# A few waits and positions moved in a projection, block-attention and linear kernel

## The reference

```
n = layernorm(x); q, k, v = n@Wq+bq, n@Wk+bk, n@Wv+bv        # split into heads
local: query block i of 128 attends to keys [128 i - 64, 128 i + 192), softmax
global: tokens {0, 62 of largest |q|, 1023} of every head attend to all 1024 keys
        and their rows replace the local ones
x = x + attention;  out = x + layernorm(x) @ (weight * scale[:, None]).T + bias
```

## Time and profile before

| | |
|---|---|
| median of three runs | 2026.45 us |
| the profiled execution, its own time | 2021.86 us |
| its span | 2020.2 us |
| PE busy (matmuls) | 1975.3 us, 98% |
| DVE busy | 1507.7 us, 75% |
| ACT busy | 1045.3 us, 52% |
| POOL busy | 543.3 us, 27% |
| granted TensorE clock, mean | 0.997 of full speed |
| one 128x512 matmul in a projection | about 0.25 us from start to start |

### The profile page before, as it was taken

How to read it: one execution, slowest core, us unless ns; L and a number is a source line. 1 busy time by engine, 2 the same in 40 slices (tenths; PEclk the granted TensorE clock), 3 DMA queues, 4 the chain that set the end, 5 groups by cost and what they waited for, 6 DMA issues and landing times.

```text
span 2020.2 us, 36804 instructions
## 1 busy us (share of the span) xinstructions
PE 1975.3 (98%) x11264; PEld 1646.0 (81%) x11264; DVE 1507.7 (75%) x2917; ACT 1045.3 (52%) x1483; POOL 543.3 (27%) x430
## 2 busy tenths in 40 slices
PE   6999999999999999999999999999999999999999
PEld 6877888888778888888788888888888888888887
DVE  5597788865877888658778887587777887666664
ACT  4326766773267667732676677327777770000100
POOL 2333123134331221243312212433222213112211
PEclk9999999999999999999999999999999999999999
DMA  3447777764377777643677776337777664333331
GB/s 126 145 113 135 157 157 159 144 126 144 119 134 158 156 161 145 123 142 122 130 161 157 161 144 125 111 92 135 157 165 172 138 149 173 125 139 132 134 127 70
DMA packets 533830, 280.79 MB, mean 139 GB/s; under 512 B 433264, under 2 KB 498870, under 8 KB 533680
## 3 DMA queue, kind: packets, MB, share of 16 engines
q1 hardware_dynamic: 505584, 186.76, 43.7%
q0 software_dynamic: 23776, 76.63, 11.7%
q10 hardware_dynamic: 4320, 15.73, 1.9%
HBM read 122.73 MB, written 51.44 MB: 86 GB/s over the span
## 4 chain that ended last, share of the span: by engine, by line
PE 62%; DVE 15%; DMA 7%; issue 7%; ACT 3%; POOL 2%; SPq 2%; DVEq 1%; ACTq 0%; POOLq 0%
PE proj L678 30%; PE proj L839 16%; PE pv L797 6%; DMA p_turned<-p_parts 5%; DVE p_parts L1564 2%; DVE top_idx L1520 2%; PE pv L819 2%; DVE x_norm L1522 2%; PE score L785 2%; PE turn L785 2%; DVE top_val L1518 1%; SPq L295 1%; PE turn L828 1%; ACT pT L1176 1%; PE proj L953 1%
## 5 line engine op out<-in xcount | busy, mean ns | idle before, releaser
L678 PE MATMUL proj<-xT_hi,w_lo 128*128 128x512 f32 x1536 | 417.6, 400 | 0.0
L678 PE MATMUL proj<-xT_hi,w_hi 128*128 128x512 f32 x1536 | 402.9, 404 | 4.9 <-POOL w_lo L468 2.4
L678 PE MATMUL proj<-xT_lo,w_hi 128*128 128x512 f32 x1536 | 385.7, 393 | 0.0
L678 PEld LDWEIGHTS proj<-xT_lo,w_hi 128*128 128x128 f32 x1536 | 291.0, 190 | 65.7 <-DVE xT_lo L1478 1.0
L1176 ACT COPY pT<-p_turned 128x1024 uint16<-128x1024 uint16 x256 | 331.7, 1373 | 21.4 <-DMA p_turned<-p_parts 21.1
L678 PEld LDWEIGHTS proj<-xT_hi,w_lo 128*128 128x128 f32 x1536 | 281.1, 190 | 58.6
L678 PEld LDWEIGHTS proj<-xT_hi,w_hi 128*128 128x128 f32 x1536 | 274.4, 188 | 63.4 <-issue 3.6
L1564 DVE COPY p_parts<-probs 128x1024 uint16<-128x1024 uint16 x320 | 225.2, 725 | 109.5 <-DMA p_turned<-p_parts 57.8
L523 POOL TENSOR_TENSOR w_lo<-w_raw,w_hi 128x1024 fp32r<-128x1024 f32 x48 | 120.2, 2505 | 593.6 <-DVE q_sq L1554 326.4
L797 PEld LDWEIGHTS pv<-v_nat,pT 128*128 128x128 f32 x2048 | 246.9, 191 | 22.5 <-issue 12.3
L797 PE MATMUL pv<-v_nat,pT 128*128 128x65 f32 x2048 | 244.2, 272 | 6.7 <-DVE ctx_out L1600 5.9
(11 more groups left out here) (181 smaller groups left out, 3173.1 us busy)
## 6 DMA issues: line engine op xcount, KB each, us to landing
w_raw<-in_wstream POOLq DMA_DIRECT2D x94, 512.0 KB, 3.7
x_buf<-in_rows SPq DMA_DIRECT2D x41, 512.0 KB, 3.3
q_rows<-pT SPq DMA_DIRECT2D x64, 256.0 KB, 2.4
ctx_rows<-ctx_out SPq DMA_DIRECT2D x128, 128.0 KB, 2.0
out<-q_store ACTq DMA_DIRECT2D x30, 512.0 KB, 2.6
q_store<-in_cols POOLq DMA_DIRECT2D x28, 512.0 KB, 5.3
q_store<-ctx_rows SPq DMA_DIRECT2D x28, 512.0 KB, 4.1
x_buf<-in_rows POOLq DMA_DIRECT2D x14, 512.0 KB, 6.5
```

What stands on the lines that cost most here:

```text
L678: mm = pe.matmul(proj[:, bank, :], w[b][:, k * P:k * P + P], x[:, k, half * HALF:half * HALF + HALF], start=(m == 0), stop=(m == 23), skip ...
```

## The change

It does five things, and no arithmetic is changed.

1. The POOL wait `parted_p(n, 0, 0)` ahead of `split_pair(n, "k", 1)` is gone, in all four batches.
2. The POOL wait `parted_p(n, PAIRS - 2, 2)` ahead of the bias additions is gone (batch 3).
3. The two `normalise` of the ahead tiles stand one place earlier in pair 6 (batch 3).
4. `ahead_hi(0)` on ACT stands behind `join_p(n, 6, 3)`, and `ahead_lo(0)` on DVE behind `columns(4)` (batch 3).
5. `spread_stats` issues both broadcasts in one place, ahead of `store_ctx(n, 3, 1)` and `turn_p(n, 3, 4)`, and waits for the whole of `top_rows` (batches 0 to 2).

```diff
         AHEAD_AT = {(5, 0): ("add", 0), (5, 1): ("moments", 0), (5, 3): ("add", 1), (5, 4): ("moments", 1),
-                    (6, 0): ("roots", 0), (6, 1): ("roots", 1), (6, 3): ("normalise", 0), (6, 4): ("normalise", 1)}
+                    (6, 0): ("roots", 0), (6, 1): ("roots", 1), (6, 2): ("normalise", 0), (6, 3): ("normalise", 1)}
...
-            def spread_stats(n, i):
-
-                if i == 0:
-                    sp.wait_ge(stat_out, n * 64 + 64)
-                    apart(sp)
-                    sp.wait_ge(top_step, n * (2 * TOP_LINKS) + TOP_LINKS + TOP_STEPS)
-                    apart(sp)
-                sp.dma_start((mean_b, rstd_b)[i], stat_rows[n, i].partition_broadcast(P)).then_inc(stat_in, 16)
+            def spread_stats(n):
+
+                sp.wait_ge(stat_out, n * 64 + 64)
+                apart(sp)
+                sp.wait_ge(top_step, (n + 1) * (2 * TOP_LINKS))
+                apart(sp)
+                for i, dst in enumerate((mean_b, rstd_b)):
+                    sp.dma_start(dst, stat_rows[n, i].partition_broadcast(P)).then_inc(stat_in, 16)
...
                 if hp == HALF_PAIRS - 1:
                     if following:
-                        spread_stats(n, 0)
+                        spread_stats(n)
                     else:
                         spread_scale(n)
                 store_ctx(n, hp, 1)
                 turn_p(n, hp, STEPS)
-                if hp == HALF_PAIRS - 1 and following:
-                    spread_stats(n, 1)
                 store_ctx(n, hp, 2)
...
                 load_columns(n, 0)
-                parted_p(n, 0, 0)
                 split_pair(n, "k", 1)
                 gather(n, 0)
...
                     pool.wait_ge(bias_in, 16)
-                    parted_p(n, PAIRS - 2, 2)
                     for b in range(AHEAD):
                         add_bias_ahead(n, b)
...
                 columns(4)
+                join_p(n, hp, STEPS - 1)
                 if early and not following:
                     ahead_hi(0)
-                join_p(n, hp, STEPS - 1)
                 out("k", 1, 3)
...
                 pv_out(u, 2)
+                columns(4)
                 if hp == PAIRS - 2 and not following:
                     ahead_lo(0)
-                columns(4)
                 if not last:
                     k_lo_out(n, hp + 1, 1)
```

## The result

The changed kernel takes 2041.52 us (median of 6 runs, 2035.65 to 2047.75), the kernel before 2025.90 in 6 runs beside it: ratio 1.0079, 95% interval 1.0056 to 1.0100. That is slower by 0.79%, outside the predicted range and on the side that had a chance of 0.12. The profiled execution took 2047.63 us with a span of 2046.0, the slow end of its kernel's own spread, against 2021.86 and 2020.2 before, the fast end of that one's: its 25.8 us are more than the 15.6 between the medians.

A forecast was written before the change was run, and what follows sets the result against it. The prediction took PE's own stream in program order (busy 1975.3 of 2020.2 us) to bound the kernel. Its terms, -0.3 + 0 + 2.4 + 1.6 + 0 = +3.7 us, gave a median of 2030.1 us, range 2019 to 2039.

The forecast's parts named there:

- What bounds it: Whole kernel: PE's stream in program order sets the time; edits count only through PE's waits and the clock behind them.
- Part 1: POOL wait removed at the start of attention, batches 0 to 2: -0.3 us, bounds -3.2 to +6.8.
- second rival: Start of attention: POOL takes the port before DVE's copies, second copy 3.4 us late; +11.8 us, 2038.3 in all; chance 0.13.
- about equally near: Batches 1 and 2, start of attention: wait's gain won, or DVE's copies delayed up to 3.4 us; taken as nothing.
- some 1 to 2: Start of attention: of a 3.4 us delay of DVE's second copy, 1 to 2 us would be seen at PE.
- Part 2: POOL wait removed ahead of batch 3's bias additions: 0 for PE, -0.7 to +0.9 us shift for later operations.
- they meet the two copies of pair 6, step 1: Batch 3: the earlier bias additions may make a second DVE copy 2 us late, hidden from PE.
- The expected gain: Batch 3: DVE's column scale no longer loses 1.9 us to the bias additions and takes 1.22 us.
- Part 3: Ahead tile in batch 3: ahead_lo(0) ends later, so PE's ahead projection starts 2.4 us later; bounds +0.5 to +3.3.
- Part 4: Second statistics broadcast beside the transposes of turn_p(3, 4): 0 us, bounds -0.4 to +1.0 in each of three batches.
- so a microsecond more should be hidden: Transposes of turn_p(3, 4): a microsecond's delay is hidden, as PE needs the result only mid-step 1 of the next pair.
- The clock: Behind PE's new 2.8 us wait at batch 3's ahead projection: one fall of the clock, +1.6 us, bounds 0 to 1.7.

The follow-up runs named there:

- e1: Kernel before without its POOL wait at the start of attention, nothing else changed: 2030.07 against 2024.85 us, ratio 1.0023.
- e7: Kernel before with the POOL wait ahead of batch 3's bias additions set on the end of DVE's small layer norm operations: 2026.45 against 2026.51 us, ratio 1.0002.
- e3: Kernel before with only ahead_hi(0) moved behind join_p(3) and ahead_lo(0) behind columns(4): 2028.57 us, ratio 1.0016.
- e2: Kernel before without its POOL wait ahead of the two bias additions of batch 3, nothing else changed: 2030.83 us, ratio 1.0027.
- e4: Kernel before with both statistics broadcasts issued in one place, the old looser wait for top_rows kept: 2027.44 us, ratio 1.0017.
- e8: Kernel before with pair 0's row moments on DVE moved behind pv_out(2): 2022.05 against 2025.36 us, ratio 0.9978.
- e9: Kernel before with pair 0's row moments behind pv_out(2), first POOL wait gone and key split ahead of load_columns: 2020.01 against 2025.36 us, ratio 0.9973.
- e5: Kernel before with its first POOL wait gone and the key split moved ahead of load_columns: 2026.47 against 2026.51 us, ratio 1.0003.
- e6: Changed kernel with the two layer norms of the ahead tiles back in their old places: 2042.77 us, ratio to the kernel before 1.0081.

## Why the prediction was wrong

**What bounds it** held: PE's stream in order, and waits with clock falls behind them. The sum of terms was wrong, +3.7 against +15.6.

**Part 1** was costed at -0.3, and measured +4.7 alone. The mechanism, its place and its size were in the text (3.4 us late; it was 3.0), as the second rival, with 0.13. The failed step is the choice between two cases "about equally near": I set batches 1 and 2 at nothing. But the choice was not open in that way: I had taken a tenth of a microsecond as what decides, and in batch 0 POOL won although the first copy's record starts 0.41 us ahead of the cast's. With two POOL operations against two copies, the offsets that the traces show, from 0.41 us one way to 0.11 the other, all collide. Batch 0 itself I had priced at a gain of 0.3 to 0.7, from copies that are nearly done when POOL comes free; they had hardly begun. What PE sees in batch 1 is two waits for `pT`, 1.34 and 1.56, in place of one of 1.84 for `q_pad`, and a longer fall of the clock, together 1.8 us of the 3.0 by which the copies are late. In batch 2 the changed kernel's trace shows next to nothing and e1's 2.7, so how much comes through differs by the execution; on the mean the "some 1 to 2" of the prediction fits the 4.7 us of e1 for three batches.

**Part 2** was costed at 0 (-0.7 to +0.9), and measured +5.5 alone. This is the largest miss. The step that failed is "they meet the two copies of pair 6, step 1". I had their new start right (1591.4), and then set it against the copies, which begin 1.8 us later, and not against the row at 1591.01: `ln_bits`, one of the operations that stand ahead of `maxima`. e7, which lets this stage of small operations pass first, has none of the loss. The expected gain did come: the column scale takes 1.22 us.

**Part 3** held: "PE starts at about 1622.2 instead of 1619.79: +2.4 us", and +1.6 for the clock, 4.0 together. e3 measured 2.3 more waiting, one fall, +4.1 in its trace and 3.2 us (1.0 to 5.5) in the medians' ratio. In the whole change the wait is 1.99.

**Part 4** was costed at 0 (up to +1.0 in each batch), and measured +3.4 alone. The place was right: the global product, which reads `pT_g`, stands in the middle of the next pair's step 1, and it is what waits. The failed step is "so a microsecond more should be hidden": the prediction shows no row of PE for it. In the trace of before the copy ends at 305.46 + 2.87 = 308.33 and PE is at this product at 308.92, so 0.6 us could be hidden. The transposes came about 1.9 us later (2.04 us of idle time on ACT against 0.16), so 1.3 was left in each batch.

**The clock** was given one fall in the sum, for the longest new wait alone. In their profiles e2 and e3 each have a fall of 3.4 us behind their new wait, and the falls of e1 are longer (17.0 us at half clock in all against 10.2); e4 has none behind its new waits.

**Open.** The 5.1 us in pair 1 of batch 2 stand behind the transpose that landed late (DVE waited 6.88 us for it). Of the eleven traces four have such a wait in this place: the changed kernel, e2 (6.56), e8 (6.17) and e9 (4.83). e2 touches nothing before batch 3, so I take it for something that comes in some executions of any of these kernels, and not for a cost of the change; that, and why it comes, was not tried. The last 3.1 us have a fall of 6.8 us at 1682.6 behind waits of 0.87 and 0.73 us, which the trace of before has alike, without a fall. Both belong to the 25.8 us of the two traces, and not for certain to the 15.6 between the medians.

## What to carry to other kernels

A wait of one engine may stand for two things, data and distance; before it goes, lay the operations that it will let loose over the other engine's rows at the new start time, by what stands in the row at that microsecond, the 0.17 us ones first, and with half a microsecond of slack either way. Follow a delayed result to the matmul that reads it, and take the difference of the two times for what can be hidden. Where waits of PE come in a cluster, taking the first away can give nothing (e5), where taking away the one behind it, which brings the clock down, does (e8).

## What the runs showed of the hardware

A 128x2 operation of DVE, 0.17 us long by itself, was held 5.15 us by two POOL additions in a row (e2 and the changed kernel alike; 5.17 in e6), though its record starts 0.37 us ahead of the first, so it would have been over. In both kernels, and at the copy of batch 0 (155.15), the held operation starts while POOL issues a DMA and the holding one is next behind that issue (155.56, 1604.38). In the traces of before and of e7 `ln_bits` started inside the same kind of issue, with POOL's next operation still waiting for a semaphore, and took 0.17. It looks as if POOL's next operation claims the port before its record starts; only these rows speak for it. The section that the prediction cites (the Trainium skill, SBUF — State Buffer, "Who interferes with whom") says that whoever issues first gets the ports; the prediction put that as whoever starts first, and by these rows the start in the record doesn't settle it. Nor is it settled who gets in between: at 1602.70 DVE's column scale got in between the same two additions, after 3.16 us, and `ln_bits` didn't.

The clock fell from the level of 2.4 to that of 1.2 GHz behind a single wait of 1.60 us (at 169.8 in e4), and not behind others of 1.31 and 1.78 us (at 311.3 and 1028.4 in the changed kernel). The falls last 3.4 or 6.8 us. The same two waits of 0.87 and 0.73 us at the end of attention had a fall behind them in four traces (the changed kernel, e2, e4 and e6) and none in the other seven; a price for a single wait can therefore only be a mean over executions.
